# Two-layer attention kernel on one core: the next pair's softmax, its copies back and its weight transposes put earlier at the end of the last window row

## The reference

```python
x = x + outlook(gn(x))     # layer 0
x = x + windows(gn(x))     # layer 1

# outlook: each pixel mixes its 3x3 neighbours, with weights of its own
a = softmax((x @ W_attn + b_attn).reshape(B, H*W, 6, 9), axis=-1)
v = x @ W_v + b_v
y = einsum('bpKhd,bphK->bphd', patches_3x3(v), a)
return y @ W_proj + b_proj

# windows: attention in shifted windows of 7x7 pixels, 12 heads of 16
q, k, v = x @ qkv_weight.T + qkv_bias
attn = softmax(q @ k.T * 16**-0.5 + rpb + mask, axis=-1)
return (attn @ v) @ proj_weight.T + proj_bias
```

## Time and profile before

| | us |
|---|---|
| median of 3 runs | 3542.67 |
| lowest and highest of them | 3532.55, 3546.12 |
| the profiled execution | 3537.01 |
| its span in the trace | 3535.2 |

### The profile page before, as it was taken

How to read it: one execution, slowest core, us unless ns; L and a number is a source line. 1 busy time by engine, 2 the same in 40 slices (tenths; PEclk the granted TensorE clock), 3 DMA queues, 4 the chain that set the end, 5 groups by cost and what they waited for, 6 DMA issues and landing times.

```text
span 3535.2 us, 105414 instructions
## 1 busy us (share of the span) xinstructions
PE 3278.2 (93%) x39908; PEld 1952.4 (55%) x39908; DVE 2756.9 (78%) x4577; ACT 1829.4 (52%) x3490; POOL 2298.3 (65%) x1889
## 2 busy tenths in 40 slices
PE   6989989899899998989989999898999999999998
PEld 3446654566445664456734666346663466634666
DVE  4978879688796887968879678786878878788786
ACT  3445644456435564456643555435654355544555
POOL 2867747677485764767657676576765777566774
PEclk7999999999999999999999999999999999999999
DMA  4742337322372323713256122561225513265122
GB/s 101 140 91 67 87 71 145 76 68 82 88 140 61 86 78 84 146 45 87 80 103 131 49 76 79 109 133 57 78 66 119 120 57 88 58 133 109 54 85 64
DMA packets 204335, 317.44 MB, mean 90 GB/s; under 512 B 16922, under 2 KB 176154, under 8 KB 203802
## 3 DMA queue, kind: packets, MB, share of 16 engines
q0 software_dynamic: 31936, 148.66, 21.6%
q1 hardware_dynamic: 171866, 161.61, 16.0%
HBM read 45.97 MB, written 38.54 MB: 24 GB/s over the span
## 4 chain that ended last, share of the span: by engine, by line
PE 32%; issue 26%; POOL 26%; DVE 6%; DMA 6%; ACT 3%; POOLq 1%; DVEq 0%; SPq 0%; ACTq 0%
POOL sp__70 L1797 10%; POOL sp__70 L1790 8%; DMA prod<-prod 5%; PE P L488 4%; POOL xw L1776 3%; DVE prod L1420 2%; POOL xr L1783 2%; PE P L493 2%; PE P L720 1%; PE P L390 1%; PE P L733 1%; PE P L506 1%; PE P L699 1%; PE P L393 1%; POOL psum_p L1726 1%
## 5 line engine op out<-in xcount | busy, mean ns | idle before, releaser
L1420 DVE TENSOR_TENSOR prod<-P,vpad 128x896 f32<-128x896 f32 (+1 forms) x768 | 790.6, 1050 | 132.0 <-PE P L488 118.3
L1797 POOL TENSOR_TENSOR sp__70<-sp__70,rc 128x588 f32<-128x588 f32 x512 | 599.8, 1173 | 437.2 <-DVE rc L1549 423.4
L1790 POOL TENSOR_TENSOR sp__70<-sp__70,mx 128x588 f32<-128x588 f32 x512 | 600.5, 1174 | 230.9 <-DVE mx L1539 230.8
L1115 ACT ACTIVATE sp__70<-sp__70 128x588 f32<-128x588 f32 x512 | 355.4, 697 | 538.0 <-POOL sp__70 L1790 537.9
L1546 DVE TENSOR_REDUCE sm<-sp__70 128x12 f32<-128x588 f32 x512 | 389.2, 760 | 255.4 <-ACT sp__70 L1115 255.3
L1532 DVE TENSOR_TENSOR sp__70<-P,relb 128x588 f32<-128x588 f32 x512 | 388.7, 761 | 180.5 <-PE P L720 171.9
L488 PE MATMUL P<-at,sel 108*128 108x448 bf16 x1512 | 425.6, 360 | 61.4 <-DVE prod L1420 31.7
L1710 POOL DMA_DIRECT2D prod<-prod x216 | 202.8, 941 | 357.9 <-DVE prod L1420 354.1
L1539 DVE TENSOR_REDUCE mx<-sp__70 128x12 f32<-128x588 f32 x512 | 388.9, 761 | 9.0
L733 PE MATMUL P<-ident,sp__70 113*98 113x113 f32 x3072 | 351.4, 265 | 20.0 <-DVE sp__70 L1532 19.4
L733 PEld LDWEIGHTS P<-ident,sp__70 113*98 113x98 f32 x3072 | 318.7, 130 | 79.6 <-issue 53.8
(11 more groups left out here) (272 smaller groups left out, 7130.7 us busy)
## 6 DMA issues: line engine op xcount, KB each, us to landing
prod<-prod POOLq DMA_DIRECT2D x216, 672.0 KB, 5.5
vbd<-vs SPq DMA_DIRECT2D x512, 147.0 KB
xin<-in_x SPq DMA_DIRECT2D x126, 336.0 KB, 5.2
out<-ot SPq DMA_DIRECT2D x184, 168.0 KB, 4.1
out<-ot SPq DMA_DIRECT2D x80, 84.0 KB
wn<-in_L_conv_qkv_weight SPq DMA_DIRECT2D x2, 432.0 KB, 6.6
wno<-in_L_conv_proj_weight SPq DMA_DIRECT2D x2, 144.0 KB, 6.7
self<-in_sel SPq DMA_DIRECT2D x3, 91.1 KB
```

The source lines that it names most:

```text
L1115: go(sp_[:, b, :], sp_[:, b, :], ACT.Exp).then_inc(p_exp, 1)
L1420: tt(by_row(dst), by_row(P[:, b:b + len(op), 0:CT]), val, ALU.mult).then_inc(prod_ok, 1)
L1790: tt(per_head(sp_[:, b, :]), per_head(sp_[:, b, :]), spread(mx[:, b, :]), ALU.subtract).then_inc(t_sub, 1)
L1797: tt(per_head(sp_[:, b, :]), per_head(sp_[:, b, :]), spread(rc[:, b, :]), ALU.mult).then_inc(p_norm, 1)
```

## The change

It moves steps within the lists of PE, ACT and DVE at the end of the last row; no instruction of work is added or removed.

- DVE: `soft_sum` goes ahead of `finish(w - 1, 2)`, and `soft_split` step 0 ahead of `wrap_out(w - 1)`; steps 1 and 2 go between the two `keep_y`.
- ACT: `back` 0 goes ahead of the last step's `keep_probs`, `back` 1 behind them, ahead of `keep_out(w - 1, 1)`; both `keep_weights` go ahead of `normalize`.
- PE: `turn_weights` part 0 goes ahead of `begin_out`, and part 1, with its wait for the copy of part 0, between `begin_out` and `end_out`.

```diff
@@ PE
                 values_middle(0)
+                turn_weights(Gn, 0, NEXT_BANK)
                 pe.wait_ge(ot_kept, ONE + NT * R)
                 begin_out(w, (R1, R2), Y_BANK)
+                pe.wait_ge(a_kept, ONE + 2 * Gn + 1)
+                turn_weights(Gn, 1, NEXT_BANK)
                 end_out(w, (R1, R2), Y_BANK)
-                turn_weights(Gn, 0, NEXT_BANK)
                 turn_out(w, 0, R1)
                 turn_out(w, 1, R2)
-                pe.wait_ge(a_kept, ONE + 2 * Gn + 1)
-                turn_weights(Gn, 1, NEXT_BANK)
                 turn_out(w, 2, Y_BANK)
@@ ACT
                     keep_out(w - 1, 0, R2)
+                    back(Gn, 0, NEXT_BANK)
                     keep_probs(w, 3, 0)
                     keep_probs(w, 3, 1)
+                    back(Gn, 1, NEXT_BANK)
                     keep_out(w - 1, 1, R1)
...
                     keep_values(Gn, 0, 0, ORDER[0], 0)
-                    back(Gn, 0, NEXT_BANK)
                     keep_values(Gn, 0, 1, ORDER[1], 0)
-                    back(Gn, 1, NEXT_BANK)
                     keep_values(Gn, 0, 2, ORDER[2], 0)
+                    keep_weights(Gn, 0, 0, NEXT_BANK)
+                    keep_weights(Gn, 0, 1, NEXT_BANK)
                     normalize(Gn + 1, 1)
-                    keep_weights(Gn, 0, 0, NEXT_BANK)
                     keep_out(w, 0, R1)
                     keep_out(w, 1, R2)
-                    keep_weights(Gn, 0, 1, NEXT_BANK)
@@ DVE
                     prob_sum(w, 3, 0)
+                    soft_sum(Gn, NEXT_BANK)
                     finish(w - 1, 2, R1)
                     prob_sum(w, 3, 1)
+                    soft_split(Gn, 0, NEXT_BANK)
                     wrap_out(w - 1)
                     keep_y(w, 2)
+                    soft_split(Gn, 1, NEXT_BANK)
+                    soft_split(Gn, 2, NEXT_BANK)
                     keep_y(w, 3)
-                    soft_sum(Gn, NEXT_BANK)
-                    for step in range(3):
-                        soft_split(Gn, step, NEXT_BANK)
```

## The result

| | before | with the change |
|---|---|---|
| median, us | 3538.25 (4 runs) | 3576.61 (4 runs) |
| lowest and highest, us | 3532.55, 3546.12 | 3565.84, 3580.57 |
| span of the profiled execution, us | 3535.2 | 3564.0 |

The ratio is 1.0098, with a 95% interval of 1.0079 to 1.0117: slower by 1%, some 35 us (the medians lie 38 apart), where 13 were forecast. The time lies above the range.

What follows compares the result with a forecast made beforehand. Bound: a PE chain behind the last `attend`, released through DVE, PE and ACT. Terms of 1.00, 0.41 and 0.20, then -0.20 and +0.19, gave +1.60 us a turn, 12.8 over 8 turns: 3556 us, range 3542 to 3570.

Steps and rivals of the forecast that it cites:

- The bound: Tail of the turn: a chain on PE once the last `attend` starts, released by a chain through DVE, PE and ACT.
- `soft_sum` ahead of `finish`: On DVE: `finish` starts 0.46 us later in a turn; the 0.60 us hole hides the rest of the 1.08.
- `soft_split` 0 ahead of `wrap_out`: On DVE: 0.61 us less 0.08 of overlap, +0.53; `wrap_out(w-1)` 0.99 late in all, POOL's second division hidden.
- `back` 0 ahead of `keep_probs`: On ACT: the copy itself costs nothing more, filling time in which ACT waited for PE; `attend` comes 1.00 us later.
- The clock: Rival, chance 0.30: more PE idle time ahead of `turn_out(w-1, 0)` lowers the clock, 1.6 us a fall; 3562 to 3568.
- The eight and four transposes: On PE in the projection: eight put into a busy list cost 0.41 us, four ahead of `end_out` 0.20.
- The new wait: PE's wait for ACT's copy of part 0, ahead of the projection's second half: hidden, with 1.1 us to spare.
- The end: Behind the projection: -0.20 us without the four transposes, +0.19 since the fourth `turn_out` needs `keep_out(w, 0)`.
- The restart follows the copies: Rival, chance 0.05: `reps` of the next turn starts 3.67 us after ACT's last weights copy; 3530, faster by 0.36%.
- three signs of being wrong: The gap ahead of `reps` shrinks, `attend` isn't later, or the clock ahead of the jump is under 1.00 in several turns.

Runs made afterwards that it cites:

- The last run: Kernel before, with DVE making both `prob_sum` of the last step ahead of `soft_max` and `soft_shift`, and PE and ACT handling its probabilities earlier: 0.9976.

## Why the prediction was wrong, step by step

**The bound** was read rightly: a chain on PE behind the last `attend`, and DVE's list ahead of it. The last run, which works on nothing else, won what that reading gives.

***`soft_sum` ahead of `finish`***, forecast +0.46: measured +0.40.

***`soft_split` 0 ahead of `wrap_out`***, forecast +0.53: the place was right (+0.55), and this is the step that failed. It priced the move of `wrap_out` by what now stands ahead of it, and took the copy's 0.14 us along unchanged. In the same step POOL's second division was said to be late by the 0.46 alone, which "hides behind that". But the copy was put behind the very reciprocal that releases this division. It now meets POOL, and waits for it and for the two memsets: +1.50 us a turn, 12 of the 35 us. The runs with a reduction (0.21 us) and with late memsets (0.83 us) show this. The Trainium skill (SBUF — State Buffer, Who interferes with whom) has a rule for it: a copy on VectorE may use the SBUF ports that it shares with GpSimd, one of the two then waits for the whole instruction of the other, and a reduction never contends on this chip. The 0.21 us agree with that, and so does 0.83; 1.64 goes beyond it, since the copy waited for three instructions and not for one. The prediction didn't weigh the rule. That it is the ports, no run here shows by itself; that it is POOL's work, they do.

***`back` 0 ahead of `keep_probs`***, forecast nothing: +0.03 where the clock stayed up (2.89 instead of 2.86 us from the copy's end to `attend`). Right. ***The clock***, a rival at 0.30, came true in all 8 turns, since the idle time was 3.4 us and not the 1.92 that I gave it. It cost 0.92 a turn (by the run with filled idle time), less than the 1.6 that I read from the restart. At 1.96 us idle, in the run with the reduction, it fell in no profiled turn, so for its own idle time the forecast's sum could leave it out. But at 1.33 us, in the run with `wrap_out` put back, it fell in one turn of 8: the length of the idle time alone doesn't decide.

***The eight and four transposes***, forecast 0.61: measured 0.97. Four ahead of `end_out` take 0.21, as forecast, but the eight put `begin_out` off by 0.64 (its first product now starts 1.02 us after the last of the values, 0.38 before), not 0.41: the first transpose behind the values and the first product behind the transposes each start later than in a run of the same kind. The other 0.12 lie behind each batch, where the first product (L650, L661) is followed by the next after 0.38 and 0.39 us instead of 0.32. So a size was wrong here, not the mechanism. ***The new wait*** costs nothing: part 1 starts 0.33 us after the product ahead of it, as `end_out` did before. ***The end***: 2.64 us, as before.

***The restart follows the copies***: falls. On ACT the copy of part 1 with the change is this:

```profile
3119.88 0.54 ACT L994 ACTIVATE at<-P 108x448 bf16<-108x448 bf16 x1 [1.73 <-PE P L436]
```

It ends 3.4 us ahead of PE's last transpose (3123.85); before it ended 0.2 us behind it. So it comes 3.7 us sooner against PE's end, and still from PE's last transpose to `reps` 3.4 to 4.2 us pass, 3.3 to 4.1 before.

With 0.40, 0.55, 0.03 and 0.97 the forecast of 1.60 would have been 1.95, 16 us, as in the run with the reduction (2.02 a turn, 1.0052). The error is the copy and what its idle time did to the clock: 2.4 us a turn. The forecast of 3556 was added to a median of three runs that lies 4.4 us above the median of four given here, so as a time it looks better by that much than it is as a loss. None of the three signs of being wrong came up: the gap ahead of `reps` stayed, `attend` was later (by 3.3 us), and the clock fell earlier than in the 12 us that were to be watched. They could not see a longer copy.

## What to carry to other kernels

When a step is moved, its own length must be priced in the new place as well: ask what each other engine does at that time, above all POOL beside a copy of DVE from SBUF to SBUF. A short instruction on the path whose release is also that of a long POOL instruction belongs ahead of that release, or can be put as another operation, as the reduction here (0.21 us beside POOL). Work that nobody waits for gains nothing by coming sooner, and pays with all that is behind it; look first for what releases the next engine, and move that.

## What the runs showed that I had not expected

The copy did not get its turn at the end of the POOL instruction in whose course it was issued: POOL's next two followed without a pause, and the copy ended with the last (1.64 us), while without them it ended with the first (0.83). Elsewhere in the kernel the same copy starts in the last 0.1 us of a POOL instruction and takes 0.16 to 0.17 us; POOL's next starts 0.05 us behind that instruction, while the memsets each start some 0.06 us before the one ahead of them ends. Whether this decides is open.

The version that beats both has the same wait in small. There the copy starts inside the second memset, takes 0.31 us instead of 0.14 and ends with it:

```profile
3070.40 0.58 POOL L1693 MEMSET vpad<- 128x336 f32 x1
3070.71 0.31 DVE L1570 COPY fin<-fin 128x63 f32<-128x63 f32 x1
```

Work added to an idle PE made the changed kernel faster: with 1.9 us of products in each turn the clock stayed at 2.4 GHz, and a turn took 0.92 us less (1.0069 against 1.0098). And in the run with late memsets 2.5 to 2.6 us of idle time brought the clock down in six turns of 8 and not in two; in four of the six it fell not at once but 1.1 to 1.5 us after PE had gone on, and stayed low into the values.
